# Linear attention with numerator and denominator in one 32-column product per head, normalised in token-major layout

## The chip, the cores and the metric

The kernel runs on one core of a Trainium2 chip. The metric is the time of one execution in microseconds (us) on the device; the figure of a kernel is the median of several runs. Engines are named PE (TensorE, matrix products and transposes), ACT (ScalarE), DVE (VectorE), POOL (GpSimd) and SP (SyncE, which issues DMAs). SBUF is the on-chip memory, PSUM the 8 banks that PE writes.

## The reference

The input `x` has 8 sequences of 512 tokens with 256 features. The output is the input plus an attention and a mixture-of-experts FFN, both on the layernormed input:

```python
xn = _layernorm(x)
x = x + attn(xn, W_qkv, proj, W_out, b_out) + ffn(xn, W1, b1, W2, b2, Wr, br)
```

The attention is linear, with 16 heads of 16 columns and 128 features a head:

```python
q_p = elu(einsum('bhnd,hdf->bhnf', q, proj)) + 1.0
k_p = elu(einsum('bhnd,hdf->bhnf', k, proj)) + 1.0
kv = einsum('bhnf,bhnd->bhfd', k_p, v)
attn = einsum('bhnf,bhfd->bhnd', q_p, kv)
k_sum = k_p.sum(axis=2)
z = 1.0 / (einsum('bhnf,bhf->bhn', q_p, k_sum) + 1e-08)
attn = attn * z[..., None]
return attn.transpose(0, 2, 1, 3).reshape(b, n, d) @ W_out.T + b_out
```

The FFN sends every token to its 2 best experts of 8 (hidden size 1024, gelu) and adds their outputs with softmax weights. All is float32.

## The kernel before, in words

**Stages.** After a setup (weights loaded and transposed, first layernorm) come 8 batches of attention, one sequence each, b = 0 to 7. While batch b is in attention, batch b+1 goes through the projections to q, k, v and the router, and batch b+2 through the layernorm statistics. Then the FFN runs over 37 tiles of 256 gathered rows, an expert after the other, with indirect DMAs that add the rows to the output.

**Order.** Every engine has its own program, and its order is written out by hand: a function `iteration(b)` for PE (line 607), one for ACT (907) and one for DVE (1236), and a loop in POOL's program (1514). Each walks through 32 units u of a batch and has its extras hung on certain units. Engines meet by semaphores that count. `feat` counts finished features, `at_rdy` finished pieces of the normalised attention, and so on.

**Units.** Unit u makes one 128x512 piece of a feature map. PE multiplies into one of four banks F0 to F3 (line 521 for u < 16, the features `kp` of the keys; line 527 for u >= 16, the features `qp` of one head of the queries). ACT takes the exponential into `e_ring` (879). DVE takes a max and a min of the two (1192). PE may start unit u when feature u-3 of DVE is done, so the three are a ring of four.

**Extras around the change.** Matrix products for the projections are three products of rounded parts (`mm3`, lines 449 to 451). The tokens of batch b+1 are transposed in two halves, `tokens_T` (479), behind units 7 and 9 of PE, into banks WK0 and WK1; ACT copies each half rounded (`tokens_hi`, 851, units 6 and 8) and DVE subtracts for the rest (`tokens_lo`, xTl, 1108, units 6 and 8). Then PE does the four q/k groups behind units 12 to 15 and the four value and router products behind units 19 to 22. `kv` (540) behind units 8, 11, 16 and 19 collects the state of batch b in the bank DEN; DVE copies it (`copy_state`, 1213, unit 19); PE transposes it behind unit 23 (549); ACT writes it into two arrays, `num_w` and `den_w`, 16 columns a head and 1 column a head, the rest zeros.

**Attention before.** For each of four groups of four heads there are two PE steps: `attn_den` (563) and `attn_num` (576), each four products of 128x32 weights by 128x512 features. The groups of heads 0 to 7 stand behind units 26 to 29, the others behind units 0, 1, 3 and 5 of the next batch. Two groups are added into one bank, one head shifted by 16 partitions. ACT copies the numerators (`copy_num`, 888). DVE adds 1e-8 to the denominators (`denominators`, 1196, unit 4), takes reciprocals in four pieces of 128x128 (1202, units 5, 7, 9, 10). PE spreads each reciprocal row over the 16 partitions of its head by a product with a 0/1 matrix (`spread`, 584, units 17, 18), and DVE multiplies (`normalise`, 1209, units 16, 17). The result lies with channels on partitions, as the output projection needs it. POOL splits it into a rounded part and a rest (1507, 1512), PE projects behind units 24 and 25, DVE adds the residual.

These are the lines of PE's order that put the transposes of the tokens in their place:

```python
                if u == 7 and not last:
                    pe.wait_ge(v_rdy, NT * b + NT)
                    wait(pe, o_rdy, 2 * b)
                    tokens_T(b + 1, 0)
                if u == 9:
                    pe.wait_ge(pos_read, b + 1)
                    if not last:
                        tokens_T(b + 1, 1)
```

## Time and profile before

| what | value |
|---|---|
| median of 3 runs | 815.17 us (813.47 to 818.41) |
| the profiled execution | 814.0 us |
| its span in the trace | 812.2 us |
| mean granted clock of PE | 0.983 |
| PE busy | 746.2 us, 92% |
| DVE busy | 558.2 us, 69% |
| ACT busy | 467.8 us, 58% |
| POOL busy | 255.5 us, 31% |

The span is what the trace covers; the execution's own time is 1.8 us longer. The shares of busy time are means over the attention stage and the FFN. All durations in the text are of the profiled execution. In a timeline, neighbours on one engine overlap a little, so that the distance of two starts, and not the duration, says how far an instruction advances its engine.

### The profile page before, as it was taken

To read this page: it belongs to the slowest core of one execution; us is meant where nothing else is said; L and a number is where in the kernel's file an instruction comes from. 1 tells how busy PE (TensorE), PEld (TensorE's weight loads), DVE (VectorE), ACT (ScalarE), POOL (GpSimd) and SP (SyncE) were. 2 spreads that over 40 slices of the span, in tenths; PEclk is the share of its full clock that TensorE was granted. 3 is DMA by queue.
4 is the path that set the end of the run, shared out by engine and by line. 5 is a ranking of instruction groups with operands and counts; after the bars stand their busy time and mean duration, and the time that the engine had idled before them with its cause. 6 is when DMAs were issued, how large, how long until landed. Compare 5 with 4: busy or idle time off the path is not lost.

```text
span 812.2 us, 19839 instructions
## 1 busy us (share of the span) xinstructions
PE 746.2 (92%) x6226; PEld 627.9 (77%) x6227; DVE 558.2 (69%) x1370; ACT 467.8 (58%) x968; POOL 255.5 (31%) x192
## 2 busy tenths in 40 slices
PE   2699999999999998799999999999999999988993
PEld 2584748474747474469999999999989999988992
DVE  8889999999999989876446464446464444646442
ACT  2466666656656566566466755457565456765542
POOL 6032525343434435112222233222233222223222
PEclk9899999999999999999999999999999999999997
DMA  6674463636363646643344322253533225352331
GB/s 158 176 199 114 132 188 100 195 92 196 91 203 84 181 103 172 234 168 74 54 133 119 73 47 50 47 138 52 138 52 49 51 43 140 53 136 47 54 53 20
DMA packets 71806, 89.57 MB, mean 110 GB/s; under 512 B 11424, under 2 KB 55136, under 8 KB 71648
## 3 DMA queue, kind: packets, MB, share of 16 engines
q1 hardware_dynamic: 57520, 70.06, 31.2%
q0 software_dynamic: 13728, 18.62, 13.2%
q10 hardware_dynamic: 528, 0.52, 0.2%
q8 instruction: 15, 0.25, 0.1%
q14 instruction: 15, 0.12, 0.0%
HBM read 38.71 MB, written 25.30 MB: 79 GB/s over the span
## 4 chain that ended last, share of the span: by engine, by line
PE 52%; DVE 19%; DMA 17%; issue 8%; ACT 2%; DVEq 1%; POOLq 0%; POOL 0%; ACTq 0%
DMA out<-ysb,icur 16%; PE F L449 5%; PE F L450 5%; PE F L451 5%; PE NUM L449 4%; PE NUM L451 4%; PE NUM L450 4%; DVE kp L1192 3%; PE F L527 3%; PE WK L449 3%; PE WK L450 2%; PE WK L451 2%; PE DEN L451 2%; PE DEN L449 2%; PE DEN L450 2%
## 5 line engine op out<-in xcount | busy, mean ns | idle before, releaser
L965 ACT ACTIVATE h<-F,b1c 128x256 f32<-128x256 f32 x296 | 131.7, 467 | 175.5 <-PE F L451 175.4
L1542 POOL DMA_INDIRECT out<-ysb,icur x74 | 118.8, 1605 | 335.1 <-DVE ysb L1390 189.8
L879 ACT ACTIVATE e_ring<-F 128x512 f32<-128x512 f32 x256 | 147.7, 608 | 56.0 <-PE F L527 35.6
L1373 DVE TENSOR_TENSOR hl<-h,hh 128x512 fp32r<-128x512 f32 x148 | 100.2, 690 | 107.2 <-ACT hh L969 105.8
L449 PE MATMUL F<-gxh,wh 128*128 128x256 f32 x592 | 169.0, 285 | 4.8 <-issue 4.8
L450 PE MATMUL F<-gxl,wh 128*128 128x256 f32 x592 | 167.7, 283 | 0.0
L451 PE MATMUL F<-gxh,wl 128*128 128x256 f32 x592 | 167.7, 283 | 0.0
L449 PEld LDWEIGHTS F<-gxh,wh 128*128 128x128 f32 x592 | 113.7, 192 | 8.1 <-issue 8.1
L450 PEld LDWEIGHTS F<-gxl,wh 128*128 128x128 f32 x592 | 113.7, 192 | 0.2 <-issue 0.2
L451 PEld LDWEIGHTS F<-gxh,wl 128*128 128x128 f32 x592 | 113.7, 192 | 0.0
L1490 POOL DMA_INDIRECT xg<-rows,slots x64 | 63.4, 991 | 143.7 <-issue 143.7
L969 ACT ACTIVATE hh<-h 128x512 fp32r<-128x512 f32 x148 | 93.5, 631 | 4.8
L1192 DVE SCALAR_TENSOR_TENSOR qp<-F,e_ring 128x512 f32<-128x512 f32 x128 | 86.9, 685 | 9.7 <-ACT e_ring L879 8.8
L449 PE MATMUL NUM<-wh,hh 128*128 128x256 f32 x296 | 86.9, 294 | 5.2 <-DVE hl L1373 5.1
L1192 DVE SCALAR_TENSOR_TENSOR kp<-F,e_ring 128x512 f32<-128x512 f32 x128 | 83.6, 666 | 1.1 <-PE DEN L540 0.4
L451 PE MATMUL NUM<-wh,hl 128*128 128x256 f32 x296 | 83.8, 283 | 0.0
L450 PE MATMUL NUM<-wl,hh 128*128 128x256 f32 x296 | 83.7, 283 | 0.0
L521 PEld LDWEIGHTS F<-stacked_proj,Sk 97*128 97x128 f32 x256 | 40.5, 193 | 46.7 <-DVE kp L1192 31.1
L449 PE MATMUL DEN<-wh,hh 128*128 128x256 f32 x248 | 70.3, 283 | 0.0
L451 PE MATMUL DEN<-wh,hl 128*128 128x256 f32 x248 | 70.3, 283 | 0.0
L450 PE MATMUL DEN<-wl,hh 128*128 128x256 f32 x248 | 70.3, 283 | 0.0
L521 PE MATMUL F<-stacked_proj,Sk 97*128 97x256 f32 x256 | 58.5, 321 | 10.2 <-DVE kp L1192 9.8
(194 smaller groups left out, 1492.5 us busy)
## 6 DMA issues: line engine op xcount, KB each, us to landing
wraw<-L_ffn_W SPq DMA_DIRECT2D x16, 1024.0 KB, 7.9
grow<-xg SPq DMA_DIRECT2D x38, 272.0 KB
Sk<-kdh SPq DMA_DIRECT2D x64, 128.0 KB, 2.3
Sq<-qdh SPq DMA_DIRECT2D x64, 128.0 KB
xin<-L_attn_x SPq DMA_DIRECT2D x8, 512.0 KB
Sk<-kdl SPq DMA_DIRECT2D x32, 128.0 KB, 2.3
Sq<-qdl SPq DMA_DIRECT2D x32, 128.0 KB
xres<-L_attn_x SPq DMA_DIRECT2D x8, 512.0 KB, 4.1
```

The costliest lines, as they stand in the source:

```text
L449: nc.tensor.matmul(dst, wh_, mh_, start=first, stop=False)
L450: nc.tensor.matmul(dst, wh_, ml_, start=False, stop=False)
L451: return nc.tensor.matmul(dst, wl_, mh_, start=False, stop=last)
L521: last = nc.tensor.matmul(F[c][:, s * D:(s + 1) * D], Sk[0:SROWS, pr, n * P:(n + 1) * P], stacked_proj[0:SROWS, 2 * pr:2 * pr + 2, :], sta ...
L527: last = nc.tensor.matmul(F[h % 4][:, :], stacked_proj[0:SROWS, h, :], Sq[0:SROWS, h // 2, :], start=True, stop=True)
L879: A(e_ring[:, u % 4, :], F[u % 4][:, :], ACT.Exp, bias=EXP_BIAS, scale=1.0 / DOWN).then_inc(exp_done, 1)
L965: A(h32[:, m, :], F[m % 4][:, 0:T], ACT.Gelu, bias=b1c[:, w, m:m + 1]).then_inc(gelu, 1)
L969: A(hh[:, 2 * q:2 * q + 2, :], h32[:, 2 * q:2 * q + 2, :], ACT.Copy).then_inc(hh_rdy, 1)
L1192: V.scalar_tensor_tensor(dst, F[u % 4][:, :], DOWN, e_ring[:, u % 4, :], ALU.max, ALU.min).then_inc(feat, 1)
L1373: V.tensor_tensor(hl[:, 2 * q:2 * q + 2, :], h32[:, 2 * q:2 * q + 2, :], f32(hh[:, 2 * q:2 * q + 2, :]), ALU.subtract).then_inc(hl_rdy, 1)
L1490: pool.indirect_dma_start(xg, bass.IndirectOffsetOnAxis(slots[:, k:k + 1], 0), rows[:, n, :], None, bounds_check=last_row, oob_is_err=Fals ...
L1542: pool.indirect_dma_start(out, bass.IndirectOffsetOnAxis(icur[:, s, :], 0), ysb[:, s, :], None, bounds_check=last_token, compute_op=ALU.ad ...
```

## The change

A head's weights for the attention are now one 32-column block `st_w`: 16 columns of state and 16 columns that all hold the sum of the key features, as the transposed state has them. One product per head (`attend`) gives numerator and denominator in 32 partitions of a bank. The four groups use the banks NUM, DEN, NUM, DEN and stand behind units 26, 28, 31 and unit 3 of the next batch. ACT copies each to SBUF and adds 1e-8 to the denominators on the way through a bias column of the constants (`copy_att`). PE transposes to token-major, four transposes for each of four groups of 128 tokens (`to_tokens`, behind units 6, 6, 8, 9). DVE takes the reciprocals of 128 tokens by 16 heads and multiplies with a broadcast operand (`reciprocals`, `products`, at units 5, 6, 8, 9), reading the bank. PE transposes back to channel-major (`to_heads`, units 17, 18); ACT rounds (`at_hi`) and DVE subtracts (`at_lo`) from that bank, and POOL does neither any more.

The second `tokens_T` moves from unit 9 to unit 10 and waits for the four products; the halves on ACT and DVE move from units 6 and 8 to 7 and 10. The copy of the state moves from DVE to ACT. Writing the state is one ACT instruction. POOL's memsets of `num_w` and `den_w` go, W_out comes by one DMA instead of four, and POOL's `sem_inc(sums)` stands before its two waits for stores. In tile 0 of the FFN the last pieces of the last batch are interleaved in the same way.

Cut to what matters:

```diff
--- before.py
+++ after.py
@@ -135,13 +132,11 @@
     kv_sb = sb("kv_sb", [P, 512], F32)
-    num_w = sb("num_w", [P, HEADS, 32], F32)
-    den_w = sb("den_w", [P, HEADS, 32], F32)
+    st_w = sb("st_w", [P, HEADS, 32], F32)
+    rec = sb("rec", [P, NT, HEADS], F32)
     r_num = place[0]
-    num_sb = sb("num_sb", [P, 2, 512], F32)
-    den_sb = sb("den_sb", [P, 512], F32)
-    rec_sb = sb("rec_sb", [P, 512], F32)
-    at = sb("at", [P, 2, 512], F32)
+    att_sb = sb("att_sb", [P, 4, 512], F32)
+    at = sb("at", [P, NT, D], F32)
     ath = sb("ath", [P, 2, 512], F32R)
@@ -197,10 +192,11 @@
     NUM, DEN = bank("NUM"), bank("DEN")
+    ATT_BANK = [NUM, DEN, NUM, DEN]
     QK_BANK = [WK[0], WK[1], NUM, WK[0]]
     V_BANK = [WK[0], WK[1], NUM, WK[0]]
-    SPREAD_BANK = [WK[1], NUM]
     PROJ_BANK = [NUM, WK[0]]
+    TOK_BANK, AT_BANK = [NUM, WK[1], NUM, WK[1]], [WK[1], NUM]
     STATE, POS = WK[1], WK[1]
@@ -533,7 +524,7 @@
                 pe.wait_ge(v_rdy, NT * b + NT)
-                wait(pe, den_read, b)
+                wait(pe, att_rdy, 4 * b)
             for c in range(4):
@@ -550,39 +541,35 @@
 
-        def attn_wait(b, g, s):
-            if s == 0:
+        def attend(b, c):
+
+            if c == 0:
                 pe.wait_ge(state_rdy, b + 1)
-            pe.wait_ge(feat, 32 * b + 20 + 8 * g + 4 * s)
-
-        def attn_den(b, g, s):
-
-            attn_wait(b, g, s)
+            else:
+                wait(pe, att_rdy, 4 * b + c - 1)
+            pe.wait_ge(feat, 32 * b + 20 + 4 * c)
             for j in range(4):
-                h = 8 * g + 4 * s + j
-                last = nc.tensor.matmul(DEN[32 * j:32 * j + 32, :], den_w[:, h, :], qp[:, h, :],
-                                        start=g == 0 and s == 0, stop=g == 1 and s == 1,
-                                        skip_group_check=True)
-            if g == 1 and s == 1:
-                last.then_inc(den_done, 1)
-
-        def attn_num(b, g, s):
-
-            attn_wait(b, g, s)
-            if s == 0:
-                wait(pe, num_rdy, 2 * b + g)
-            for j in range(4):
-                h = 8 * g + 4 * s + j
-                last = nc.tensor.matmul(NUM[32 * j:32 * j + 32, :], num_w[:, h, :], qp[:, h, :],
-                                        start=s == 0, stop=s == 1)
-            if s == 1:
-                last.then_inc(attn_done, 1)
-
-        def spread(b, g):
-
-            pe.wait_ge(rec_rdy, b + 1)
-            nc.tensor.matmul(SPREAD_BANK[g][:, :], cst[:, C_SEL + P * g:C_SEL + P * (g + 1)], rec_sb[:, :],
-                             start=True, stop=True).then_inc(spread_full, 1)
+                h = 4 * c + j
+                last = nc.tensor.matmul(ATT_BANK[c][32 * j:32 * j + 32, :], st_w[:, h, :], qp[:, h, :],
+                                        start=True, stop=True)
+            last.then_inc(attn_done, 1)
+
+        def to_tokens(b, n):
+
+            if n == 0:
+                pe.wait_ge(att_rdy, 4 * b + 4)
+            if n >= 2:
+                pe.wait_ge(at_rdy, 4 * b + n - 1)
+            for c in range(4):
+                last = nc.tensor.transpose(TOK_BANK[n][:, c * P:(c + 1) * P], att_sb[:, c, n * P:(n + 1) * P], ident)
+            last.then_inc(tok_full, 1)
+
+        def to_heads(b, g):
+
+            pe.wait_ge(at_rdy, 4 * b + 4)
+            for n in range(NT):
+                last = nc.tensor.transpose(AT_BANK[g][:, n * P:(n + 1) * P], at[:, n, g * P:(g + 1) * P], ident)
+            last.then_inc(at_full, 1)
 
@@ -610,22 +597,24 @@
                 unit(b, u)
-                if u == 0 and not first:
-                    attn_den(b - 1, 1, 0)
-                if u == 1 and not first:
-                    attn_num(b - 1, 1, 0)
                 if u == 3 and not first:
-                    attn_den(b - 1, 1, 1)
-                if u == 5 and not first:
-                    attn_num(b - 1, 1, 1)
+                    attend(b - 1, 3)
+                if u == 6 and not first:
+                    to_tokens(b - 1, 0)
+                    pe.wait_ge(pos_read, b + 1)
+                    to_tokens(b - 1, 1)
                 if u == 7 and not last:
                     pe.wait_ge(v_rdy, NT * b + NT)
                     wait(pe, o_rdy, 2 * b)
                     tokens_T(b + 1, 0)
+                if u in (8, 9) and not first:
+                    to_tokens(b - 1, u - 6)
                 if u == 8:
                     kv(b, 0)
-                if u == 9:
+                if u == 10:
                     pe.wait_ge(pos_read, b + 1)
+                    if not first:
+                        pe.wait_ge(at_rdy, 4 * b)
                     if not last:
@@ -639,7 +628,6 @@
                 if u == 14 and not last:
-                    wait(pe, num_rdy, 2 * b)
                     qk_group(b + 1, 2)
                 if u == 15 and not last:
                     pe.wait_ge(qkl_rdy, 4 * b + 5)
@@ -651,24 +639,22 @@
                         pe.wait_ge(qkl_rdy, 4 * b + 6)
                     else:
                         pe.wait_ge(pos_read, b + 2)
-                    spread(b - 1, 0)
+                    to_heads(b - 1, 0)
                 if u == 18 and not first:
                     if not last:
                         pe.wait_ge(qkl_rdy, 4 * b + 7)
-                    else:
-                        pe.wait_ge(num_rdy, 2 * b)
-                    spread(b - 1, 1)
+                    to_heads(b - 1, 1)
                 if u == 19:
                     kv(b, 3)
                     if not last:
                         v_logits(b + 1, 0)
                 if u == 20 and not last:
                     if not first:
-                        pe.wait_ge(at_rdy, 2 * b - 1)
+                        pe.wait_ge(atl_rdy, 2 * b - 1)
                     v_logits(b + 1, 1)
                 if u == 21 and not last:
                     if not first:
-                        pe.wait_ge(at_rdy, 2 * b)
+                        pe.wait_ge(atl_rdy, 2 * b)
                     v_logits(b + 1, 2)
@@ -690,18 +676,16 @@
                     project(b - 1, 1)
-                if u == 27:
+                if u == 26:
                     if first:
                         pe.wait_ge(v_rdy, NT * b + 7)
                     else:
                         pe.wait_ge(o_rdy, 2 * b + 1)
-                    attn_num(b, 0, 0)
-                if u == 26:
-                    attn_den(b, 0, 0)
+                    attend(b, 0)
                 if u == 28:
-                    attn_den(b, 0, 1)
-                if u == 29:
-                    attn_num(b, 0, 1)
+                    attend(b, 1)
+                if u == 31:
+                    attend(b, 2)
                 if u == 30:
@@ -879,26 +863,23 @@
         def at_hi(b, g):
-            act.wait_ge(at_rdy, 2 * b + g + 1)
-            A(ath[:, g, :], at[:, g, :], ACT.Copy).then_inc(ath_rdy, 1)
-
-        def copy_num(b, g):
-            act.wait_ge(attn_done, 2 * b + g + 1)
-            wait(act, at_rdy, 2 * (b - 1) + g + 1)
-            A(num_sb[:, g, :], NUM[:, :], ACT.Copy).then_inc(num_rdy, 1)
+            act.wait_ge(at_full, 2 * b + g + 1)
+            A(ath[:, g, :], AT_BANK[g][:, :], ACT.Copy).then_inc(ath_rdy, 1)
+
+        def copy_att(b, c):
+            act.wait_ge(attn_done, 4 * b + c + 1)
+            A(att_sb[:, c, :], ATT_BANK[c][:, :], ACT.Identity, bias=cst[:, C_EPS:C_EPS + 1]).then_inc(att_rdy, 1)
+
+        def copy_kv(b):
+            act.wait_ge(kv_done, NT * b + NT)
+            A(kv_sb[:, :], KV[:, :], ACT.Copy).then_inc(kv_rdy, 1)
 
         def state(b):
 
             act.wait_ge(state_full, b + 1)
-            wait(act, attn_done, 2 * b)
-            st = STATE[:, :].rearrange("p (h c) -> p h c", c=32)
-            for s in range(2):
-                A(num_w[:, :, :].rearrange("p (g s j) c -> p g s j c", s=2, j=4)[:, :, s, :, 16 * s:16 * s + HD],
-                  st.rearrange("p (g s j) c -> p g s j c", s=2, j=4)[:, :, s, :, 0:HD], ACT.Copy, scale=1.0 / DOWN)
-
-            for c in range(4):
-                last = A(den_w[:, 4 * c:4 * c + 4, c:c + 1], st[:, 4 * c:4 * c + 4, HD:HD + 1], ACT.Copy, scale=1.0 / DOWN)
-            last.then_inc(state_rdy, 1)
+            wait(act, attn_done, 4 * b)
+            A(st_w[:, :, :], STATE[:, :].rearrange("p (h c) -> p h c", c=32), ACT.Copy,
+              scale=1.0 / DOWN).then_inc(state_rdy, 1)
 
@@ -907,13 +888,17 @@
                 exp(b, u)
-                if u == 5 and not first:
-                    copy_num(b - 1, 1)
-                if u in (6, 8) and not last:
-                    tokens_hi(b + 1, (u - 6) // 2)
+                if u == 0 and not first:
+                    copy_att(b - 1, 2)
+                if u == 4 and not first:
+                    copy_att(b - 1, 3)
+                if u in (7, 10) and not last:
+                    tokens_hi(b + 1, (u - 7) // 3)
+                if u == 19:
+                    copy_kv(b)
                 if 11 <= u < 15 and not last:
                     qk_hi(b + 1, u - 11)
-                if u in (17, 18) and last:
+                if u in (17, 18) and not first:
                     at_hi(b - 1, u - 17)
@@ -925,8 +910,8 @@
                     rows_hi(0)
-                if u == 30:
-                    copy_num(b, 0)
+                if u in (27, 29):
+                    copy_att(b, (u - 27) // 2)
 
@@ -1187,30 +1173,27 @@
                 dst = qp[:, h, :]
-                if h % 8 == 0:
-                    wait(dve, attn_done, 2 * b + h // 8 - 1)
+                if h % 4 == 0:
+                    wait(dve, attn_done, 4 * (b - 1) + h // 4 + 1)
             V.scalar_tensor_tensor(dst, F[u % 4][:, :], DOWN, e_ring[:, u % 4, :], ALU.max, ALU.min).then_inc(feat, 1)
 
-        def denominators(b):
-            dve.wait_ge(den_done, b + 1)
-            V.tensor_scalar(den_sb[:, :], DEN[:, :], 1e-8 * DOWN, None, ALU.add).then_inc(den_read, 1)
-
-        def reciprocals(b, q):
-
-            dve.wait_ge(den_read, b + 1)
-            cols = slice(q * P, (q + 1) * P)
-            last = V.reciprocal(rec_sb[:, cols], den_sb[:, cols])
-            if q == 3:
-                last.then_inc(rec_rdy, 1)
-
-        def normalise(b, g):
-            dve.wait_ge(num_rdy, 2 * b + g + 1)
-            dve.wait_ge(spread_full, 2 * b + g + 1)
-            V.tensor_tensor(at[:, g, :], num_sb[:, g, :], SPREAD_BANK[g][:, :], ALU.mult).then_inc(at_rdy, 1)
-
-        def copy_state(b):
-            dve.wait_ge(kv_done, NT * b + NT)
-            V.tensor_copy(kv_sb[:, :], KV[:, :]).then_inc(kv_rdy, 1)
+        def reciprocals(b, n):
+
+            dve.wait_ge(tok_full, NT * b + n + 1)
+            heads = TOK_BANK[n][:, :].rearrange("p (h c) -> p h c", c=32)
+            V.reciprocal(rec[:, n, :], heads[:, :, HD]).then_inc(rec_rdy, 1)
+
+        def products(b, n):
+
+            dve.wait_ge(rec_rdy, NT * b + n + 1)
+            heads = TOK_BANK[n][:, :].rearrange("p (h c) -> p h c", c=32)
+            V.tensor_tensor(at[:, n, :].rearrange("p (h d) -> p h d", d=HD), heads[:, :, 0:HD],
+                            rec[:, n, :].unsqueeze(2).to_broadcast([P, HEADS, HD]), ALU.mult).then_inc(at_rdy, 1)
+
+        def at_lo(b, g):
+
+            dve.wait_ge(ath_rdy, 2 * b + g + 1)
+            V.tensor_tensor(atl[:, g, :], AT_BANK[g][:, :], f32(ath[:, g, :]), ALU.subtract).then_inc(atl_rdy, 1)
 
@@ -1243,18 +1226,18 @@
                     norm_step(b + 1, u + 10)
+                if not first and u in (5, 6, 8, 9):
+                    reciprocals(b - 1, (5, 6, 8, 9).index(u))
                 features(b, u)
                 if ahead and not last and u == 21:
                     norm_var(b + 2)
-                if u == 19:
-                    copy_state(b)
                 if not last:
                     if u == 2:
                         norm_rows(b + 1, 0, 2)
                     if u == 3:
                         norm_rows(b + 1, 2, 4)
-                    if u in (6, 8):
-                        tokens_lo(b + 1, (u - 6) // 2)
+                    if u in (7, 10):
+                        tokens_lo(b + 1, (u - 7) // 3)
                     if 11 <= u < 15:
                         qk_lo(b + 1, u - 11)
                     if u == 22:
@@ -1284,12 +1267,10 @@
                     rows_lo(0)
                     rows_tokens(0)
                 if not first:
-                    if u == 4:
-                        denominators(b - 1)
-                    if u in (5, 7, 9, 10):
-                        reciprocals(b - 1, (5, 7, 9, 10).index(u))
-                    if u in (16, 17):
-                        normalise(b - 1, u - 16)
+                    if u in (5, 6, 8, 9):
+                        products(b - 1, (5, 6, 8, 9).index(u))
+                    if u in (17, 18):
+                        at_lo(b - 1, u - 17)
                     if u in (23, 24):
@@ -1460,8 +1441,6 @@
         nc.gpsimd.memset(vext[:, :, :, HD:32], 1.0)
-        nc.gpsimd.memset(num_w[:, :, :], 0.0)
-        nc.gpsimd.memset(den_w[:, :, :], 0.0)
         nc.gpsimd.memset(rows[:, :, TOK_COL:ROWW], 0.0).then_inc(s_zero, 1)
...
```

How the order moves on DVE, units 7 to 9. Before (names: `kp` a feature, `den_sb` and `rec_sb` denominators and reciprocals, `xTl` the rest of the tokens):

```order
L1192 SCALAR_TENSOR_TENSOR kp_102<-F2,e_ring_90 128x512
L1108 TENSOR_TENSOR xTl_107<-WK0,xTh_106 128x512
L1181 REGISTER_ALU
L1192 SCALAR_TENSOR_TENSOR kp_102<-F3,e_ring_90 128x512
L1202 RECIPROCAL rec_sb_96<-den_sb_95 128x128
L1181 REGISTER_ALU
L302 REGISTER_ALU
L1192 SCALAR_TENSOR_TENSOR kp_102<-F0,e_ring_90 128x512
L1107 REGISTER_ALU
L1108 TENSOR_TENSOR xTl_107<-WK1,xTh_106 128x512
```

After (`at` the products, `rec` the reciprocals):

```order
L1178 SCALAR_TENSOR_TENSOR kp_100<-F3,e_ring_90 128x512
L1093 ISA
L1094 TENSOR_TENSOR xTl_105<-WK0,xTh_104 128x512
L1182 REGISTER_ALU
L1184 RECIPROCAL rec_93<-NUM 128x16
L1167 REGISTER_ALU
L297 REGISTER_ALU
L1178 SCALAR_TENSOR_TENSOR kp_100<-F0,e_ring_90 128x512
L1190 TENSOR_TENSOR at_95<-NUM,rec_93 128x256
L1182 REGISTER_ALU
L1184 RECIPROCAL rec_93<-WK1 128x16
L1167 REGISTER_ALU
```

The 128x128 reciprocals have gone, small reciprocals stand ahead of a feature and the products behind it, and the first xTl is one feature later; the second xTl (bank WK1) is further behind.

How the order moves on PE, units 8 to 12. Before (L479 is `tokens_T`, L540 `kv`, L521 a unit, L449 the first q/k product):

```order
L521 MATMUL F0<-stacked_proj_61,Sk_108 128x256 x2
L540 MATMUL DEN<-kp_102,vext_103 32x128 x16
L302 REGISTER_ALU
L521 MATMUL F1<-stacked_proj_61,Sk_108 128x256 x2
L479 MATMUL WK1<-cst_49,xn_66 128x128 x4
L302 REGISTER_ALU
L521 MATMUL F2<-stacked_proj_61,Sk_108 128x256 x2
```

After (L564 is `to_tokens`, L470 `tokens_T`, L531 `kv`, L512 a unit):

```order
L512 MATMUL F0<-stacked_proj_61,Sk_106 128x256 x2
L562 REGISTER_ALU
L564 MATMUL NUM<-cst_49,att_sb_94 128x128 x4
L531 MATMUL DEN<-kp_100,vext_101 32x128 x16
L297 REGISTER_ALU
L512 MATMUL F1<-stacked_proj_61,Sk_106 128x256 x2
L564 MATMUL WK1<-cst_49,att_sb_94 128x128 x4
L297 REGISTER_ALU
L512 MATMUL F2<-stacked_proj_61,Sk_106 128x256 x2
L470 MATMUL WK1<-cst_49,xn_66 128x128 x4
```

The transposes of the tokens into WK1 have moved past one more unit and stand behind the transposes of the attention into the same bank.

## Rows read from the trace of the kernel before

**Rows 1.** Windows: length, busy time by engine, PEclk, DMA; three batches, then one batch in three.

```profile
...
73.30:192.71 119.41, 114.77 (x1001) 72.67 (x993) 112.57 (x304) 73.51 (x167) 49.18 (x42) 1.00 0.54 148
...
192.71:203.13 10.42, 8.79 (x102) 5.32 (x98) 10.42 (x20) 6.43 (x12) 7.04 (x8) 1.00 0.82 232
203.13:216.50 13.37, 13.37 (x116) 10.17 (x117) 12.20 (x21) 6.98 (x15) 6.13 (x5) 1.00 0.52 127
216.50:232.51 16.01, 16.01 (x118) 8.71 (x116) 14.95 (x61) 10.95 (x30) 3.23 (x3) 1.00 0.39 107
...
```

**Rows 2.** Timeline of DVE in that batch: start, duration, instruction, [idle before].

```profile
...
197.21 0.67 DVE L1196 TENSOR_SCALAR den_sb<-DEN 128x512 f32<-128x512 f32 x1
197.81 0.67 DVE L1192 SCALAR_TENSOR_TENSOR kp<-F,e_ring 128x512 f32<-128x512 f32 x1
198.41 0.94 DVE L1202 RECIPROCAL rec_sb<-den_sb 128x128 f32<-128x128 f32 x1
199.27 0.62 DVE L1192 SCALAR_TENSOR_TENSOR kp<-F,e_ring 128x512 f32<-128x512 f32 x1
...
202.41 0.67 DVE L1108 TENSOR_TENSOR xTl<-WK,xTh 128x512 fp32r<-128x512 f32 x1
...
216.50 0.69 DVE L1192 SCALAR_TENSOR_TENSOR qp<-F,e_ring 128x512 f32<-128x512 f32 x1 [0.89 <-ACT e_ring L879]
...
```

**Rows 3.** Timeline of PE in that batch.

```profile
...
199.39 0.60 PE L479 MATMUL WK<-cst,xn 128*128 128x128 f32 x4
199.94 0.50 PE L521 MATMUL F<-stacked_proj,Sk 97*128 97x256 f32 x2
...
201.56 1.08 PE L540 MATMUL DEN<-kp,vext 128*32 128x128 f32 x32
...
203.13 0.50 PE L449 MATMUL WK<-xTh,WTh 128*128 128x512 f32 x1
...
210.86 0.50 PE L527 MATMUL F<-Sq,stacked_proj 97*128 97x512 f32 x1
211.20 1.02 PE L584 MATMUL WK<-rec_sb,cst 128*128 128x512 f32 x2
...
212.29 1.02 PE L584 MATMUL NUM<-rec_sb,cst 128*128 128x512 f32 x2
...
218.47 0.60 PE L549 MATMUL WK<-cst,kv_sb 128*128 128x128 f32 x4
218.83 0.48 PE L527 MATMUL F<-Sq,stacked_proj 97*128 97x512 f32 x1
...
222.46 1.07 PE L563 MATMUL DEN<-qp,den_w 128*32 128x512 f32 x8
223.45 0.51 PE L527 MATMUL F<-Sq,stacked_proj 97*128 97x512 f32 x1
...
```

**Rows 4.** Groups by form: count, busy in all, mean ns of one, idle before.

```profile
...
L1388 DVE TENSOR_TENSOR ytmp<-NUM,b2bc 128x256 f32<-128x256 f32 x37 | 15.6, 422 | 4.1 <-PE NUM L451 3.9
...
L1150 DVE RECIPROCAL erec<-esum 128x4 f32<-128x4 f32 x8 | 1.4, 178 | 0.3
...
```

**Rows 5.** Timeline of DVE near the end of batch 6.

```profile
...
308.20 0.69 DVE L1192 SCALAR_TENSOR_TENSOR qp<-F,e_ring 128x512 f32<-128x512 f32 x1 [0.73 <-ACT e_ring L879]
...
```

**Rows 6.** Timeline of the setup, POOL and DVE.

```profile
...
3.66 0.53 POOL L1463 MEMSET num_w<- 128x512 f32 x1
...
4.77 3.51 POOL L1467 MEMSET Sk<- 1x4096 f32 x1
...
6.06 2.25 DVE L1084 TENSOR_SCALAR var<-mv 128x4 f32<-128x4 f32 x1
...
```

**Rows 7.** Timeline of DVE in the last batch, token counts.

```profile
...
322.72 1.99 DVE L1315 CAST counts_i<-counts 1x8 int32<-1x8 f32 x1
...
```

**Rows 8.** Windows before the batches, columns as in rows 1.

```profile
...
34.00:36.00 2.00, 0.15 (x4) 0.18 (x4) 1.76 (x14) 0.23 (x1) 0.00 (x0) 1.00 0.88 204
38.00:40.00 2.00, 2.00 (x6) 1.49 (x6) 2.00 (x5) 1.66 (x4) 0.75 (x1) 0.50 0.88 201
...
```

More of the change, by code:

```diff
@@ L61, in constants @@
     c[:, C_PAD:C_PAD + SUB] = p[:, None] + P * np.arange(SUB) + TOKENS
-    for g in range(2):
-        for r in range(P):
-            c[32 * (r // 32) + 2 * g + (r % 32) // 16, C_SEL + P * g + r] = 1.0
+    c[:, C_EPS] = 1e-8 * DOWN * (p % 32 >= HD)
     return c
@@ L1519, in _ @@
             add_bias(b - 1)
-            for g in range(2):
-                at_hi(b - 1, g)
-                at_lo(b - 1, g)
             copy_rows(b + 1)
@@ L1525, in _ @@
         add_bias(NB - 2)
-        for g in range(2):
-            at_lo(NB - 2, g)
         add_bias(NB - 1)
```

76 lines of the change are left out of this document (33 added, 43 removed).

## The prediction

> **What bounds the kernel now.** I read the engine totals first, then the windows of one batch, then the timelines of DVE and PE inside it, and only then the groups.
>
> The FFN half does not change: its 37 tiles begin after the last batch and PE does not wait there. So the question is the length of a batch, times the number of batches. The windows say that a batch lasts 39.8 us (119.41 / 3, and again 39.80 as the sum of the three stretches from 192.71 to 232.51) and that no engine fills it: PE is busy 38.17 us of it, DVE 37.57, ACT 24.36 [rows 1]. Both PE and DVE have holes, so neither's sum alone gives the period; they hand it to each other. That is what the three stretches show. In the first, from the first feature of a batch (f0, 192.71) to the start of the q/k projection of the next batch (203.13), DVE is busy 10.42 of 10.42 and PE 8.79. In the second, up to the feature of unit 19 (216.50), PE is busy 13.37 of 13.37 and DVE 12.20. In the third both are full or nearly (PE 16.01, DVE 14.95 of 16.01) [rows 1].
>
> The hand-overs are in the timelines. DVE works through features and extras without a gap; the last extra that somebody waits for is `tokens_lo` of the second half at 202.41 (xTl), and PE's first `mm3` on it starts at 203.13, 0.72 after [rows 2, 3]. From there PE runs without a gap until the first value projection, and DVE then waits 0.89 at unit 19 for the exponential that follows it on ACT [rows 2]. So the loop is: f0 → DVE to tokens_lo(1) → PE to unit 20 → ACT → f19 → both to the next f0. A change moves the time by what it does to these legs, not by what it does to a sum.
>
> **Prices.** On DVE a full-width (128x512) instruction advances the engine by 0.60 us (197.21 → 197.81 → 198.41), a 128x128 reciprocal by 0.86 (198.41 → 199.27) [rows 2]. Removed per batch: one denominator add, four reciprocals, two normalisations, one state copy: 0.60 + 4 x 0.86 + 2 x 0.60 + 0.60 = 5.84 us. Added: four reciprocals of 128x16, four products of 128x256, two 128x512 subtractions. Reciprocals: 128x4 costs 178 ns [rows 4] and 128x128 940 ns [rows 2], so 6.1 ns an element more; 16 elements are 0.25 us, of which 0.17 advance the engine (0.08 overlap, as 0.94 against 0.86). Products: a two-operand 128x256 from PSUM takes 422 ns [rows 4], 0.36 of advance. This one reads 16 of every 32 columns and a broadcast operand; the trace has no such access, so its bounds are 0.30 (256 elements at the rate of the 128x512 one, half of 0.60) and 0.68 (if it costs like the 512 columns it spans). I take 0.36. Sum added: 4 x 0.17 + 4 x 0.36 + 2 x 0.60 = 3.3. DVE gets 2.5 us less per batch.
>
> On PE an attention group advances the engine by 0.99 (222.46 → 223.45); a spread costs 1.09 - 0.34 = 0.75 (211.20 → 212.29, less the unit between, 210.86 → 211.20); a set of four transposes costs 0.36 (218.47 → 218.83) to 0.55 (199.39 → 199.94) [rows 3]. Removed: four groups and two spreads, 5.5 us. Added: six sets of transposes, 2.2 to 3.3. PE gets 2.2 to 3.3 us less. The four removed groups lie in the third stretch and at the start of the first; the transposes lie in the first (four sets) and second (two). ACT gets eight 128x512 instructions (four attention copies, two copies of the heads, one before and one after the state's transposes) for two copies and six small ones; it is busy 24.36 of 39.8 [rows 1], so its sum does not decide. POOL's two pairs of operations go; nobody waited for POOL in the loop.
>
> **The legs after the change.**
>
> Leg 1, f0 to the start of qk. Up to unit 4 DVE is as before (f4 at +3.90). Then, from the order of the changed kernel, reciprocal, feature, product for units 5, 6, 8 and 9, tokens_lo(0) behind unit 7: +4.50 recip(0), 4.67 f5, 5.27 product(0), 5.63 recip(1), 5.80 f6, 6.40 product(1), 6.76 f7, 7.36 tokens_lo(0), 7.96 recip(2), 8.13 f8, 8.73 product(2), 9.09 recip(3), 9.26 f9, 9.86 product(3), ends 10.28. PE's second tokens_T is now behind unit 10 and waits for all four products, because they read its bank WK1. It starts at 10.33; before, it started at 6.68 (199.39 - 192.71). Queued behind it on PE: unit 11, kv(1), unit 12 and the qk products. Transposes 0.55, unit 0.35, kv about 1.0 (32 pieces, 1.08 busy [rows 3]), unit 0.35: qk starts at 12.66 by PE's queue. By the other way, ACT's copy and tokens_lo(1) on DVE are done at 12.33, so PE's own queue decides, just. Before it was 10.42. Leg 1: +2.24. So DVE does less and yet the leg is longer: before, the transposed tokens lay ready for DVE from ACT long before their turn in its queue at +9.70 (202.41); a start 3.65 us later uses that slack up and more, since it now hangs on the previous batch's normalisation.
>
> Leg 2, qk to f19. PE is continuous there (13.37 of 13.37), so it shortens by PE's saving: two spreads become two sets of transposes of 0.36 to 0.55 each, 2 x (0.75 - 0.41) = 0.68. 13.37 becomes 12.69. at_hi and at_lo behind units 17 and 18 lie in the place of the normalisations (0.60 each).
>
> Leg 3, f19 to the next f0, 16.01 us. The state copy leaves DVE (-0.60) and goes to ACT, which there is between the exponentials and the value copies on which DVE waits; I price the exchange at zero, bounds -0.6 and +0.6. Attention: PE has three groups here instead of four, but DVE is the engine with the unbroken queue in this leg, and its list is otherwise unchanged. Zero.
>
> Period: 39.80 + 2.24 - 0.68 = 41.36, **+1.56 us**.
>
> **The sum.** Batches 1 to 5: 5 x 1.56 = +7.8. Batch 6: +1.56, less 0.73 of wait for e_ring at unit 30 [rows 5] that two fewer groups ahead of it should remove: +0.8. Batch 0 has nothing of an earlier batch, but tokens_T(1) still is one unit later: +0.5. Setup: the first layernorm instructions on DVE end with POOL's long memsets (L1084, 2.25 us from 6.06, ends 8.31; Sk ends 8.28) and POOL reaches these about 2 x 0.47 us earlier without its memsets of num_w and den_w (0.53 for num_w, den_w is as large, and neighbours overlap a little) [rows 6]: -0.95, up to -2.3 if an instruction slips ahead of a memset. Last batch: DVE has 2.5 less, but the token counts end behind a POOL addition, whatever DVE does (L1315, 1.99 us for 8 numbers [rows 7]); I keep -0.9 (bounds 0 and -2.5). Hand-over into the FFN: fewer products in tile 0, -0.2. Sum: 7.8 + 0.8 + 0.5 - 0.95 - 0.9 - 0.2 = +7.05. The profiled execution took 814.0 and spans 812.2; it becomes 821. The median of the runs is 815.17, so the median becomes 822.2; I say 822.
>
> What the Trainium skill adds, in "SBUF — State Buffer", section "Who interferes with whom": the pair of ports that DVE and GpSimd share is an exclusive lock, held for a whole instruction by whoever issues first, and taken by DVE's copy, cast and tensor_scalar in 2-port mode; a DVE instruction with at most one SBUF input outside those modes does not contend. The trace agrees at the setup (2.25 us for 128x4, as long as the memset lasts) and at the token counts. By that rule, taking at_hi and at_lo away from GpSimd buys nothing in the loop beyond its own work, as DVE's features there read PSUM and one SBUF operand; the sum stays as it is.
>
> **Rivals.**
>
> A, faster: the sums set the period. If PE is not held at the second tokens_T (because product(3) is early, or the queue behind it fills the gap), leg 1 falls with DVE's saving: it would be 10.42 less about 1.7, and legs 2 and 3 less 0.7. Period about 37.4, -2.4 x 6.5 batches = -15.6: 799. For it: DVE and PE are both over 94% busy and both lose over 2 us. It decides where the second tokens_T starts by 8.8 (10.33 - 1.56): from there on the period is no longer than before. Against it: the wait for four products is in the code, and the fourth stands behind ten features in DVE's unbroken queue.
>
> B, slower: the strided products are dear. At 0.68 each, products (0) to (3) delay tokens_T(1) by 4 x 0.32 = 1.3 us, a little of it hidden; +1.04 x 6 = +6 on top: 828. It decides from 0.41 of advance (0.47 busy) on: the 1.1 us from 822.2 to 823.3 are 24 products by 0.046. Place: DVE units 5 to 9. For it: no row has a half-filled read. Against: DVE's rows otherwise go by elements.
>
> C, slower: TensorE's clock. PE would idle about 2 us ahead of the second tokens_T (unit 10 is issued by about 8). Before the batches (34 to 40 us), a stretch with PE busy 0.15 of 2.00 us is followed by one at 0.50 granted, 1.2 GHz [rows 8]; in the batches the clock is 1.00 (2.4 GHz) throughout [rows 1]. If it falls, PE's next stretch of some 3 us doubles: +3 x 6, 840. Against it: in the new gap PE still has units 8 to 10 to do.
>
> D, in between: the gap is partly filled, or the setup gives 2 us more: leg 1 only +1.2 makes 0.5 a batch; with the setup at -0.95 or -2.3 the total is 815 to 817. For it: PE's units 8 to 10 and four sets of transposes have to fit somewhere, and may come later than I let them; against it: DVE's list, which sets 10.28, doesn't ask for PE.
>
> **How the numbers follow.** A measurement of this kernel tells about 1% from no change (807.0 and 823.3). My forecast (819 to 826) has 0.52, A 0.17, B 0.13, C 0.06, D 0.12. Of my forecast two thirds lie below 823.3. Faster by over 1%: 0.17, A. Within 1%: 0.33 + 0.12 = 0.45. Slower: 0.19 + 0.13 + 0.06 = 0.38. The range leaves out C and half of A and of B's upper end: 803 to 829; the forecast's own is 819 to 826.
>
> **What would show it.** In the profile after: products of about 0.42 us on DVE; PE idle of 1.5 to 2.5 us ahead of the second tokens_T in every batch, with DVE's `at` as releaser; qk 12.7 us after f0; unit 19 at 25.4; period 41.4. I am wrong if the second tokens_T waits for nothing, if the period is below 39.8, or if the third stretch moves by more than 0.6 either way.

## The result, and the profile after

The changed kernel takes 820.16 us (median of 20 runs, 815.1 to 825.3), the kernel before 816.06 (20 runs, 812.85 to 819.67). The ratio is 1.0048, interval 1.0029 to 1.0068: slower by half a per cent, about 4 us. The profiled execution took 818.8 us and spans 816.9.

The windows of one batch, with the edges at the same events as [rows 1] (first feature, start of the q/k products, feature of unit 19, which is now at 217.33, first feature of the next batch):

```profile
192.81:204.89 12.08, 9.20 (x110) 6.78 (x107) 11.28 (x27) 6.11 (x11) 8.70 (x9) 1.00 0.72 210
204.89:217.33 12.44, 12.44 (x122) 10.10 (x120) 9.56 (x17) 7.88 (x17) 2.58 (x2) 1.00 0.44 100
217.33:233.44 16.11, 13.97 (x90) 8.51 (x93) 14.42 (x61) 12.16 (x28) 0.00 (x0) 0.97 0.46 127
```

Leg 1 is 12.08 long where it was 10.42, leg 2 12.44 where it was 13.37, leg 3 16.11 where it was 16.01. The batch takes 40.63 instead of 39.80. In it PE is busy 35.61 us (38.17 before) and DVE 35.26 (37.57): both do over 2 us less and the batch is 0.83 longer. That is what a sum of work cannot show.

The timelines of DVE and PE where leg 1 ends, answering to [rows 2, 3]:

```profile
201.21 0.40 DVE L1190 TENSOR_TENSOR at<-NUM,rec 128x256 f32<-128x256 f32 x1
201.53 0.24 DVE L1184 RECIPROCAL rec<-WK 128x16 f32<-128x16 f32 x1
201.70 0.62 DVE L1178 SCALAR_TENSOR_TENSOR kp<-F,e_ring 128x512 f32<-128x512 f32 x1
202.24 0.40 DVE L1190 TENSOR_TENSOR at<-WK,rec 128x256 f32<-128x256 f32 x1
202.57 0.67 DVE L1178 SCALAR_TENSOR_TENSOR kp<-F,e_ring 128x512 f32<-128x512 f32 x1
204.04 0.69 DVE L1094 TENSOR_TENSOR xTl<-WK,xTh 128x512 fp32r<-128x512 f32 x1 [0.80 <-ACT xTh L835]
```

```profile
202.75 0.63 PE L470 MATMUL WK<-cst,xn 128*128 128x128 f32 x4 [1.58 <-issue]
203.13 0.48 PE L512 MATMUL F<-stacked_proj,Sk 97*128 97x256 f32 x2
203.54 1.08 PE L531 MATMUL DEN<-kp,vext 128*32 128x128 f32 x32
204.55 0.51 PE L512 MATMUL F<-stacked_proj,Sk 97*128 97x256 f32 x2
204.89 0.40 PE L440 MATMUL WK<-xTh,WTh 128*128 128x512 f32 x1
```

The fourth product ends at 202.64; 0.1 later PE begins the second `tokens_T` after 1.58 us of idle time. The view puts "issue" beside this idle time and names no releaser. Of the waits that stand there in the code, the one on `at_rdy`, for the fourth product, is the only one that had not been met earlier, and its time fits. Before, ACT's rounded half had been ready at 200.62 and DVE took it up without a wait at 202.41; now DVE waits 0.80 for it.

Over five batches (1 to 5) the difference adds up to 4.06 us:

```profile
71.00:273.63 202.63, 179.13 (x1599) 128.33 (x1595) 176.22 (x516) 131.16 (x276) 56.41 (x50) 0.98 0.53 144
```

(198.57 us from 73.30 to 271.87 before.) Its PEclk is 0.98, against 1.00 before: TensorE is at times at 1.2 GHz inside batches 1 to 6, which it never was in the profile before. The start of such a stretch, and the six microseconds ahead of it:

```profile
226.00:228.00 2.00, 1.47 (x9) 0.53 (x5) 1.86 (x10) 2.00 (x5) 0.00 (x0) 1.00 1.01 333
228.00:230.00 2.00, 1.69 (x11) 0.61 (x11) 1.90 (x8) 1.12 (x3) 0.00 (x0) 1.00 0.54 191
230.00:232.00 2.00, 1.23 (x6) 0.62 (x5) 1.84 (x8) 1.65 (x4) 0.00 (x0) 1.00 0.83 191
232.00:234.00 2.00, 1.70 (x10) 0.57 (x10) 1.61 (x11) 1.09 (x3) 0.00 (x0) 0.62 0.87 200
```

In the kernel before, PE was busy 2.00 of 2.00 in the first three of these windows, and its clock stayed at 1.00 in all four.

The setup, answering to [rows 6]. The first feature comes at 34.43 instead of 37.25:

```profile
3.66 0.13 POOL L1444 MEMSET rows<- 128x32 f32 x1
3.85 3.51 POOL L1446 MEMSET Sk<- 1x4096 f32 x1
```

```profile
6.02 1.36 DVE L1070 TENSOR_SCALAR var<-mv 128x4 f32<-128x4 f32 x1
7.42 3.44 DVE L1072 TENSOR_SCALAR rbits<-var 128x4 int32<-128x4 int32 x1
```

The first two tiny DVE operations still end with the memsets (7.38 and 7.36), only 0.92 earlier. The third, `rs<-rbits`, does not. Before, it ran from 11.82 beside POOL's third memset and took 1.85 us; now POOL waits 0.41 for a DMA ahead of that memset, and DVE is through before it starts:

```profile
10.89 0.17 DVE L1074 TENSOR_SCALAR rs<-rbits 128x4 int32<-128x4 int32 x1
11.25 1.80 POOL L1449 MEMSET praw<- 1x2048 f32 x1 [0.41 <-DMA praw<-L_attn_proj]
```

So the normalised tokens xn, the next step, start at 12.86 instead of 15.48, which is 2.62 of the 2.82. In the last batch the token counts still stand behind POOL, as in [rows 7]:

```profile
323.81 2.26 DVE L1296 CAST counts_i<-counts 1x8 int32<-1x8 f32 x1
```

### The profile page after: what moved, and what is told of

Read it like the earlier page. It is cut to its first block, busy times and chain, and to the rows that moved or that the text cites. A ratio compares the mean times of both kernels' runs of the same rounds, so it can differ in the third digit from the quotient of the medians.

```text
span 816.9 us, 19638 instructions
## 1 busy us (share of the span) xinstructions
PE 730.6 (89%) x6130; PEld 642.7 (79%) x6131; DVE 535.0 (65%) x1384; ACT 481.5 (59%) x964; POOL 223.4 (27%) x164
## 4 chain that ended last, share of the span: by engine, by line
PE 46%; DVE 20%; DMA 18%; issue 11%; ACT 3%; DVEq 1%; POOLq 0%; POOL 0%; ACTq 0%
DMA out<-ysb,icur 17%; PE F L440 4%; PE F L442 4%; PE F L441 4%; DVE qp L1178 4%; PE DEN L531 4%; PE NUM L440 3%; PE NUM L442 3%; PE NUM L441 3%; PE F L512 3%; PE DEN L442 2%; PE DEN L441 2%; PE DEN L440 2%; PE WK L440 2%; DVE kp L1178 2%
## 5 line engine op out<-in xcount | busy, mean ns | idle before, releaser
L1506 POOL DMA_INDIRECT out<-ysb,icur x74 | 121.0, 1635 | 336.3 <-DVE ysb L1371 190.8
L863 ACT ACTIVATE e_ring<-F 128x512 f32<-128x512 f32 x256 | 149.6, 611 | 63.4 <-PE F L512 33.8
L512 PEld LDWEIGHTS F<-stacked_proj,Sk 97*128 97x128 f32 x256 | 42.0, 203 | 36.4 <-DVE kp L1178 15.6
L512 PE MATMUL F<-stacked_proj,Sk 97*128 97x256 f32 x256 | 61.3, 334 | 10.4 <-DVE qp L1178 6.1
```

What stands on the lines that cost most here:

```text
L512: last = nc.tensor.matmul(F[c][:, s * D:(s + 1) * D], Sk[0:SROWS, pr, n * P:(n + 1) * P], stacked_proj[0:SROWS, 2 * pr:2 * pr + 2, :], sta ...
L863: A(e_ring[:, u % 4, :], F[u % 4][:, :], ACT.Exp, bias=EXP_BIAS, scale=1.0 / DOWN).then_inc(exp_done, 1)
L1506: pool.indirect_dma_start(out, bass.IndirectOffsetOnAxis(icur[:, s, :], 0), ysb[:, s, :], None, bounds_check=last_token, compute_op=ALU.ad ...
```

## The experiments

All are edits of the changed kernel; ratios are to the kernel before, run on the same chip beside it.

**The wait for the fourth product.**

```diff
-    TOK_BANK, AT_BANK = [NUM, WK[1], NUM, WK[1]], [WK[1], NUM]
+    TOK_BANK, AT_BANK = [NUM, WK[1], NUM, NUM], [WK[1], NUM]
...
-                if u == 10:
+                if u == 9:
                     pe.wait_ge(pos_read, b + 1)
                     if not first:
-                        pe.wait_ge(at_rdy, 4 * b)
+                        pe.wait_ge(at_rdy, 4 * b - 2)
```

(The second half of the tokens on ACT and DVE goes from unit 10 to 9, the fourth `to_tokens` behind unit 11, its reciprocal and product to unit 10, and the third qk group waits for all four products.)

> The fourth set of attention transposes goes to bank NUM behind unit 11, so the second tokens_T stands behind unit 9 again and waits for the second product only. Theory (the wait for the fourth product lengthens leg 1): qk starts 11.0 us after the first feature instead of 12.1, the period falls from 40.6 to about 39.6, the whole by 5 to 6 us against the changed kernel (about 814). Rival (the longer period comes from elsewhere, for instance from the copy of the state on ACT): the period stays at 40.6 and the time at 819 to 820.

Measured: 814.02 us, ratio 0.9965 (0.9945 to 0.9984), so 0.8% below the changed kernel, 6 to 7 us. The q/k products start 10.78 us after the first feature (11.0 expected). Two batches in a row:

```profile
111.14:150.48 39.34, 35.59 (x323) 25.24 (x319) 35.19 (x104) 26.12 (x55) 11.25 (x10) 1.00 0.54 148
150.48:189.81 39.33, 35.62 (x323) 25.24 (x319) 35.19 (x103) 26.12 (x55) 11.31 (x10) 1.00 0.55 148
```

and the PE timeline from the second tokens_T (L470) to kv, now with no wait ahead of the second tokens_T:

```profile
118.66 0.60 PE L470 MATMUL WK<-cst,xn 128*128 128x128 f32 x4
119.01 0.71 PE L512 MATMUL F<-stacked_proj,Sk 97*128 97x256 f32 x4
119.99 0.66 PE L564 MATMUL NUM<-cst,att_sb 128*128 128x128 f32 x4 [0.27 <-DVE at L1192]
120.57 1.08 PE L531 MATMUL DEN<-kp,vext 128*32 128x128 f32 x32
```

The same work with that wait moved is 1.3 us a batch shorter, and shorter than before the change. All of it lies in leg 1 (10.78 instead of 12.08); the other two legs together stay at 28.56 (28.55 in the changed kernel). The hold-up of the second tokens_T is the cause of the longer batch. The edit takes away two things at once, the wait (1.58 us of idle time) and the place behind one more unit: the second tokens_T starts 2.4 us earlier, at +7.52 instead of +9.94. The two were not tried apart.

**The copy of the state.** Only `copy_kv` goes back from ACT to DVE behind unit 19.

> Only the copy of the state goes back from ACT to DVE behind unit 19. Theory (exchange at zero, as priced): period 40.6 within 0.2, time 819 to 821. Rival (the copy on ACT holds up the exponentials that DVE waits for at unit 21, 0.64 us): period 40.1 or less, time 816 to 817.

Measured: 820.48, ratio 1.0036 (1.001 to 1.0061). The undisturbed batch took 40.50. The exchange is worth 0.1 us a batch, and the rival's 40.1 did not come. The profile also has a batch of 42.39 us with the clock at 0.89 (next experiments):

```profile
112.25:152.75 40.50, 35.56 (x319) 25.54 (x319) 35.78 (x104) 25.84 (x54) 11.23 (x10) 0.99 0.53 144
152.75:195.14 42.39, 38.86 (x327) 28.08 (x319) 36.18 (x104) 26.43 (x55) 11.23 (x10) 0.89 0.52 138
```

**The setup.**

> Two memsets of 128x512 on POOL are back in the setup, into st_w and a part of att_sb. Theory (the memsets are worth their 0.95 us): the first feature comes 0.9 to 1.0 us later than the 34.4 to 35.4 us of the kernels without them, the time rises by 1. Rival (the setup's larger gain comes from the clock between 16 and 24 us, which the memsets decide): the first feature comes 2 to 3 us later, with a granted clock of about 0.5 there.

> W_out is loaded by four DMAs of 64-byte pieces as before; its rows then lie in the former order of channels, so the output projection multiplies other pairs. Theory (the memsets make the setup's gain): first feature within 0.3 us of 34.4, time the same. Rival (the small pieces delayed the loads behind them and the transposes of the weights, and with them the clock): the first feature comes 1 to 2 us later, with a granted clock of about 0.5 between 16 and 24 us.

The memsets: 822.5 us, ratio 1.0082 (1.0055 to 1.011). The first feature comes at 36.76. In the eight profiles here that have the new setup unchanged (on ordinary chips) it came at 34.4 to 35.4, so the memsets cost some 1.9 us, twice what the theory gave; PEclk was 1.00 from 16 to 24 us, so the rival's mechanism isn't it. The four DMAs: first feature at 36.00, about 1.1 later, again with PEclk 1.00; time 820.33, ratio 1.0049 (1.0026 to 1.0072), no difference in the whole. Neither expectation was met as written.

What both edits change is the third small operation. With the two memsets POOL comes to its third long memset 0.11 us before DVE comes to `rs<-rbits`; with the four DMAs POOL no longer waits for `praw` and starts the memset 0.01 after it. Both times the operation takes as long as the memset. The rows of the two, first the memsets, then the four DMAs:

```profile
11.71 1.82 POOL L1451 MEMSET praw<- 1x2048 f32 x1
11.82 1.74 DVE L1074 TENSOR_SCALAR rs<-rbits 128x4 int32<-128x4 int32 x1
```

```profile
10.90 1.84 DVE L1078 TENSOR_SCALAR rs<-rbits 128x4 int32<-128x4 int32 x1
10.91 1.80 POOL L1453 MEMSET praw<- 1x2048 f32 x1
```

In the eight profiles POOL waits 0.41 to 1.10 for `praw` there, the operation takes 0.17, and xn starts at 12.86 to 12.88. It starts at 15.36 with the memsets and at 14.54 with the four DMAs: each edit costs about 1.6 us through this one instruction, and the memsets 0.9 more by their length. From xn to the first feature the profiles differ by up to 1 us among themselves (e1_nowait has PEclk 0.59 from 16 to 24 us and its first feature at 35.40), so the first feature shows it less cleanly. Each of the two edits has one profile.

The profile with the memsets also has TensorE's clock down in every batch from 1 to 6, and each is 0.3 us or more longer. Two of them:

```profile
114.88:155.81 40.93, 37.64 (x324) 27.53 (x319) 35.44 (x104) 26.30 (x55) 11.32 (x10) 0.92 0.52 143
155.81:196.78 40.97, 37.64 (x327) 27.52 (x319) 35.45 (x104) 26.30 (x55) 11.38 (x10) 0.92 0.53 142
```

That the memsets bring this isn't shown. The mean granted clock of this kernel's nine runs is 0.950 to 0.977, that of the changed kernel's twenty 0.951 to 0.977, and the execution that was profiled had 0.959, where the profiled one of the changed kernel had 0.975.

**More room in leg 1.**

> As the kernel without the wait, but the third and fourth sets of reciprocals and products stand at units 10 and 12 of DVE, and the fourth set of transposes behind the first q/k group of PE. Theory (leg 1 is bound by DVE's list up to the second tokens_lo, and leg 2 has idle time of DVE that holds the rest): leg 1 loses another 0.5 to 0.8 us, leg 2 gains at most 0.4, period 39.0 to 39.2 against 39.3, time about 812 to 813. Rival (PE's queue of kv and units sets leg 1, not DVE): period 39.3 to 39.7, time 814 to 816.

Measured: 820.48, ratio 1.0049; period 40.64. My edit had put the fourth product behind the subtraction for kdl, and PE waited for it at the third qk group:

```profile
207.52 0.50 PE L440 MATMUL NUM<-xTh,WTh 128*128 128x512 f32 x1 [1.51 <-DVE at L1194]
```

The next order mends this.

> As e5_defer, but each product stands right behind its feature, ahead of the subtraction for q and k (kdl), for which the fourth product had waited while PE waited 1.51 us for it. Theory: PE's wait at the third q/k group goes, f16 comes 19.6 us after f0 instead of 21.1, the period is 39.1 to 39.3, the time 1.4 x 6 below e5_defer, about 812 to 813. Rival (PE's own list sets leg 2 and the wait was idle time that moves elsewhere): period 40 or more.

> The kernel of e7_early once more, since on the chip of that call PE lost some 7 us a batch in every kernel, in gaps between the single instructions of kv. Theory, as there: f16 comes 19.6 us after f0, the period is 39.1 to 39.3, the time about 812 to 813 where the kernel before takes 816 to 817. Rival (PE's own list sets leg 2): period 40 or more, time 817 or more.

The first run was on a chip where every kernel, that before too, took 50 us more or above: 872.78 against 869.48, ratio 1.0033. The second took 814.82 against 815.76, ratio 0.9986 (0.9962 to 1.0011). Here the wait is 0.23, and the undisturbed batch 39.37, no better than 39.33 without the deferring. The feature of unit 12 comes 0.75 us earlier (+12.95, not +13.70) and the four units behind it take 0.77 longer: PE's list has a set of transposes more there, and that this list takes the gain back is my reading. The theory's 39.1 to 39.3 was missed, and so was the rival's 40 or more, which was right in kind only.

**The clock.** First, PE's idle time ahead of the second tokens_T filled with repeated transposes:

> The changed kernel, with 12 transposes that only repeat the first tokens_T (same data into WK0, once DVE has read it) put into PE's idle time ahead of the second tokens_T. They are done before the fourth product ends, so the order of the path is untouched. Theory C (PE's idle time there, 1.6 us a batch, lets the granted clock fall now and then, and the falls cost 2 to 3 us on average): the mean granted clock rises from 0.968 to 0.975 or more, and the median falls by 2 to 4 us below the changed kernel's 820.2. Rival (the clock falls for another reason, or the falls cost nothing): clock and time as in the changed kernel within 1 us, or later by the added work.

They ran (1.47 us, x12) and left 0.22 of idle time. The falls stayed; the mean granted clock was 0.967. The median was 817.74, ratio 1.001 (0.9984 to 1.0036), which is below the changed kernel's but not clear of it. That gap isn't what lets the clock fall: three falls between 190 and 282 us are left in the profile. Next, PE's work near the end of a batch:

```diff
-            for j in range(4):
+            for j in [0, 1, 2, 3] * (2 if c < 3 else 1):
                 h = 4 * c + j
```

> The changed kernel, with the four products of the first three attention groups of a batch issued twice (the same values written again), so that PE has in the last units of a batch about the work that it had before. Theory C2 (PE's idle time around units 26 to 31, 2.6 us more than before, lets the granted clock fall at the end of a batch and in the next one's first stretch): the mean granted clock rises from 0.968 to 0.976 or more, the falls between 70 and 290 us go, and the time falls to 816 to 818 although PE does more. Rival (the falls cost nothing or have another cause): clock as in the changed kernel, time 820 to 823.

> The kernel of e8_twice once more, for the same reason. Theory C2 (PE's idle time around units 26 to 31 lets the clock fall): mean granted clock 0.976 or more, no falls between 70 and 290 us, time 816 to 818. Rival: clock 0.968, time 820 to 823.

The first was on the slow chip (884.83, ratio 1.0156). The second: 821.44, ratio 1.0078 (1.0048 to 1.0108), mean granted clock 0.981 to 0.982 in its four runs, where the changed kernel has 0.968 and the kernel before 0.981. PE is busy 2.00 of 2.00 again in the windows from 104 to 110 us, near the end of batch 1, and no fall is left between 70 and 290 us:

```profile
104.00:106.00 2.00, 2.00 (x18) 0.72 (x18) 1.86 (x11) 1.20 (x4) 0.00 (x0) 1.00 0.64 225
106.00:108.00 2.00, 2.00 (x18) 0.71 (x14) 1.93 (x8) 1.26 (x4) 0.00 (x0) 1.00 0.96 297
108.00:110.00 2.00, 2.00 (x18) 0.56 (x12) 1.81 (x8) 1.47 (x3) 0.00 (x0) 1.00 0.32 74
112.23:152.85 40.62, 37.11 (x347) 25.80 (x343) 35.27 (x103) 26.17 (x56) 11.24 (x10) 1.00 0.52 143
152.85:193.47 40.62, 37.13 (x347) 25.80 (x343) 35.28 (x103) 26.19 (x56) 11.26 (x10) 1.00 0.52 144
```

So the cause of the falls is shown, and half of the theory with it; but the period is the same 40.62 and the time isn't less. The doubled products cost 2.9 us in the last batch (its last feature comes at +40.76 instead of +37.87) and 1.1 in batch 6 (39.39 instead of 38.25), which blurs this. The last run leaves them out in the last batch, on the better order:

> The order of e1_nowait, with the four products of the first three attention groups issued twice (the same values again) in batches 0 to 6, not in the last. e1_nowait took 0.9965 (0.9945 to 0.9984) of the kernel before, with a mean granted clock of 0.968. Theory (the falls of the clock at the start of a batch cost 1 to 2 us in all, and idle time of PE in units 26 to 31 brings them): no falls between 70 and 300 us, clock 0.978 or more, ratio 0.993 to 0.996, and every period within 0.1 of 39.35. Rival (the falls lie where PE has slack and cost nothing on average, or the doubled products cost as much as they save): the falls go, but the ratio stays at 0.9965 or rises.

Measured: 813.68 us, ratio 0.9962 (0.9945 to 0.9979), median clock 0.981, no falls between 70 and 300 us, batches of 39.33. Without the doubling it was 0.9965 with a clock of 0.969. Doubling wins no time that can be measured, as the rival said. That the falls cost nothing doesn't follow: batch 6 again takes 1.1 us more with the doubling (38.07 instead of 36.98), so they may cost 1 to 2 us that the doubling takes back, and the two intervals, about 1.5 us to either side each, can't tell.

> The order of e7_early and the doubled products of e8_twice together. If both theories hold, the gains add up: period 39.1 to 39.3 with a granted clock of 0.976 or more, time 808 to 811. If doubling delays the path of the attention copies, it is as e7_early or 1 us above it.

This one ran on the slow chip alone: 876.13, ratio 1.0076 (1.0055 to 1.0096), 3.4 us above e7_early there. The clock rose (0.951, against 0.939), and the gains did not add up.

## Why the prediction was right, and where its sizes were off

I said 822, range 803 to 829, slower by 0.9%; measured 820.2, slower by 0.5%, which by my own 1% is no difference. The mechanism was the one named, with the 1.58 us of idle time inside my 1.5 to 2.5, and taking it away turned the sign.

That the time came so near is in part luck. In the profiled executions the stages up to the FFN are only 1.05 us longer, where my sum had 7.25 without its hand-over term of -0.2: the loop was priced too dear and the setup too low. The other 3.65 us are in the FFN, for which I had forecast nothing.

- **Leg 1**, predicted +2.24, measured +1.66. This is the term that matters in the sum. The fourth product began at +9.43, not +9.86. A product advanced DVE by 0.33 instead of 0.36, and the feature ahead of it by 0.54 rather than 0.60. The set of four transposes then advanced PE by 0.38, not 0.55.
- **Leg 2**, predicted -0.68, measured -0.93. A set of transposes there advances PE by 0.36, not 0.41, which is 0.1 of it; the rest was not traced.
- **Leg 3**, predicted 0, measured +0.10; the copy of the state alone is worth that 0.1.
- **Period**: +0.83 instead of +1.56. In five batches 4.06, not 7.8.
- **Batch 0**: 36.05 became 36.57, +0.5 as predicted. **Batch 6**: 38.56 became 38.25, -0.3 where I had +0.8; the wait at unit 30 went, as said.
- **Setup**: -2.8 in this profile, and -1.9 to -2.9 in the others, where the sum had -0.95 and the bound -2.3. I priced the memsets' length and gave the slip of an instruction ahead of a memset as a bound only. The slip is what came: `rs<-rbits` takes 0.17 instead of 1.85, and e4_wo4 shows that the four small DMAs, to which I gave nothing though the diff had them, decide it too.
- **Last batch** up to the first FFN product: 38.30 became 37.90, -0.4 instead of -0.9.
- **FFN**: predicted no change, yet in the two profiled executions it ends 3.65 us later in relation to its start. The code is the same, and the loss comes in steps, at one load of rows and in stretches with the clock down, as a PE row and two windows of the changed kernel show:
```profile
460.34 0.66 PE L590 MATMUL WK<-cst,grow 128*128 128x128 f32 x4 [1.17 <-DMA grow<-xg]
```

```profile
608.00:612.00 4.00, 4.00 (x23) 4.00 (x22) 2.11 (x6) 0.00 (x0) 1.55 (x1) 0.58 0.28 33
727.00:731.00 4.00, 3.65 (x18) 3.66 (x19) 2.45 (x4) 2.53 (x4) 0.92 (x2) 0.57 0.29 33
```

The 4 us from 608, mostly at half the clock, are 23 products where a full window elsewhere has 36. In the other nine profiles from ordinary chips, all with the same FFN, it took from 0.6 to 6.2 us longer than in the one profile of before, whose execution took 814.1 us, 2 under its median. That all ten are on one side speaks against scatter alone. With one profile of before it can't be told apart, and whether the change has a part in it stays open.

Rival B falls by one row: the product with its half-filled read costs 408 ns, a little under the 422 of the plain 128x256 form, and advances DVE by 0.33, where the rival needed 0.41.

```profile
L1190 DVE TENSOR_TENSOR at<-NUM,rec 128x256 f32<-128x256 f32 x16 | 6.5, 408 | 0.1
...
L1184 DVE RECIPROCAL rec<-NUM 128x16 f32<-128x16 f32 x16 | 3.9, 244 | 0.8 <-PE NUM L564 0.8
```

Rival C had the clock right and the rest wrong: falls did come, but at the end of a batch and not in the gap ahead of tokens_T. They reach into the first stretch of the next, where DVE is busy 11.28 of 12.08 us. A fall added from nothing (the batch from 233.44 on, in which the fall at 232 us reaches, is longer than before by the same 0.83 as the others) to 1.9 us (the 42.39 above), not 3 each; the 3 had no row behind it. Rival A's condition was the start of the second tokens_T by +8.8; e1_nowait puts it at +7.5 and the time at 0.9965, so A was right about the sign, but it was 3 us and not 16: leg 1 stays at 10.78, 0.36 above the kernel before, where A had 1.7 below it. Rival D came half true: the setup gave its 2 us and more, and leg 1's +1.66 lies between its 1.2 and my 2.24.

On the rule of the Trainium skill ("SBUF — State Buffer", "Who interferes with whom") that the port pair shared by DVE and GpSimd is an exclusive lock for a whole instruction, the trace agrees again: the operations at 6.02 and 7.42 end with the memsets, and `rs<-rbits` takes 0.17 us when it is done before POOL's next memset starts and 1.74 to 1.85 us when the two overlap.

## What to carry to other kernels

Where two engines hand a loop to each other, price a change by the legs between their hand-overs and ask for each moved step which bank or buffer it takes over and whose last reader it now waits for. Here at least 2.3 us less work on each of the two busiest engines made each batch 0.8 us longer, and one bank assigned differently, with the steps moved that this sets free, made it 0.5 shorter than it had been. In a setup, ask which small instruction meets which memset: one that slipped ahead was worth 1.6 us, more than the two memsets of 0.5 us that were removed.
